# The second value tile of a pair: projected in the step of the causal attention product instead of the step of the first two mixes

## What is computed

```python
def _L0_attn_ref(x, WQ, WK, WV, WO):          # 16 heads of width 16, causal
    Q, K, V = (heads(WQ), heads(WK), heads(WV))
    score = jnp.einsum('bhqd,bhkd->bhqk', Q, K) / jnp.sqrt(jnp.asarray(D_K, x.dtype))
    score = score + mask
    ...
    out = jnp.einsum('bhqk,bhkd->bhqd', score, V)
    ...
    return out @ WO

def _moe_attn(x, Wq, Wk, Wv, Wo, Wsel_v, Wsel_o):   # 16 heads of width 64, 8 experts, top 2
    q = _rope(jnp.einsum('bsd,hdp->bhsp', x, Wq))
    k = _rope(jnp.einsum('bsd,hdp->bhsp', x, Wk))
    gv = _gate(x, Wsel_v)
    v = jnp.einsum('bsd,bhse,hedp->bhsp', x, gv, Wv)
    att = jax.nn.softmax(jnp.einsum('bhsp,bhtp->bhst', q, k) / np.sqrt(P), axis=-1)
    o = jnp.einsum('bhst,bhtp->bhsp', att, v)
    go = _gate(x, Wsel_o)
    return jnp.einsum('bhsp,bhse,hepd->bsd', o, go, Wo)
```

## Time and profile before

| | |
|---|---|
| time, median of 3 runs | 3404.29 us (3403.39 to 3406.31) |
| span of the profiled execution | 3401.4 us |
| TensorE matmul busy | 3233.1 us, 95% |
| VectorE, ScalarE, GpSimd busy | 72%, 58%, 42% |
| mean granted TensorE clock | 0.995 of full speed |
| DMA | 295.18 MB, mean 87 GB/s |

### The profile page before, as it was taken

How to read it: one execution, slowest core, us unless ns; L and a number is a source line. 1 busy time by engine, 2 the same in 40 slices (tenths; PEclk the granted TensorE clock), 3 DMA queues, 4 the chain that set the end, 5 groups by cost and what they waited for, 6 DMA issues and landing times.

```text
span 3401.4 us, 64468 instructions
## 1 busy us (share of the span) xinstructions
PE 3233.1 (95%) x18240; PEld 2378.9 (70%) x18240; DVE 2439.7 (72%) x4708; ACT 1961.5 (58%) x4509; POOL 1441.9 (42%) x1215
## 2 busy tenths in 40 slices
PE   1699999999999999999999999999999999997998
PEld 1577777777777777777777777777777777775765
DVE  6577777777777777777777777777777777775554
ACT  2466666656666666666666666666666666664121
POOL 4144355445443454345543554434534543442212
PEclk9999999999999999999999999999999999999999
DMA  5223333334233333233233332333332433333221
GB/s 165 76 71 87 95 90 85 77 76 109 76 84 87 84 98 81 75 100 96 69 87 76 96 98 77 76 104 81 84 87 68 114 81 75 84 75 110 72 83 62
DMA packets 115937, 295.18 MB, mean 87 GB/s; under 512 B 33856, under 2 KB 54592, under 8 KB 99264
## 3 DMA queue, kind: packets, MB, share of 16 engines
q1 hardware_dynamic: 115904, 294.78, 32.9%
HBM read 262.74 MB, written 31.98 MB: 87 GB/s over the span
## 4 chain that ended last, share of the span: by engine, by line
PE 85%; issue 6%; DVE 5%; ACT 3%; DMA 1%; POOL 0%; ACTq 0%; SPq 0%; DVEq 0%; POOLq 0%
PE bank L673 27%; PE bank L799 22%; PE bank L718 9%; PE bank L773 7%; PE bank L688 5%; PE bank L905 4%; PE bank L897 3%; PE bank L693 3%; PE bank L745 2%; PE bank L754 2%; ACT probs L957 2%; DVE uf L1239 1%; DVE oo L1232 1%; PE bank L694 1%; ACT pt_e L977 1%
## 5 line engine op out<-in xcount | busy, mean ns | idle before, releaser
L573 POOL TENSOR_TENSOR u_l<-uf,u_h 128x512 fp32r<-128x512 f32 x512 | 716.1, 1409 | 722.6 <-ACT u_h L1041 722.4
L1136 DVE TENSOR_REDUCE nmax<-bank 128x1 f32<-128x512 f32 (+3 forms) x1024 | 551.8, 579 | 305.0 <-PE bank L688 297.8
L673 PE MATMUL bank<-wv_h,xx 128*128 128x512 f32 x2048 | 755.0, 410 | 7.1 <-DVE vm L1157 7.1
L957 ACT ACTIVATE probs<-bank,nmax 128x512 f32<-128x512 f32 (+3 forms) x1024 | 590.7, 610 | 253.2 <-DVE nmax L1136 253.1
L1041 ACT ACTIVATE u_h<-uf 128x512 fp32r<-128x512 f32 x512 | 321.7, 632 | 696.9 <-DVE uf L1239 683.6
L673 PEld LDWEIGHTS bank<-wv_h,xx 128*128 128x128 f32 x2048 | 386.0, 188 | 155.8 <-issue 59.6
L718 PEld LDWEIGHTS bank<-ident_sb,probs 128*128 128x128 f32 x3328 | 388.3, 141 | 106.4 <-issue 51.3
L718 PE MATMUL bank<-ident_sb,probs 128*128 128x128 f32 x3328 | 451.3, 274 | 1.6 <-ACT stackT L1032 0.9
L569 POOL TENSOR_TENSOR v_sb<-v_next,zero_hb 128x512 f32<-128x512 f32 x64 | 74.2, 1160 | 891.9 <-PE bank L773 877.4
L799 PE MATMUL bank<-u_h,wo_h 128*128 128x512 f32 x1024 | 427.1, 417 | 5.0 <-ACT u_h L1041 3.2
L1239 DVE TENSOR_TENSOR uf<-oo,go 128x512 f32<-128x512 f32 x512 | 416.2, 823 | 8.8 <-POOL u_l L573 6.6
(11 more groups left out here) (141 smaller groups left out, 5164.2 us busy)
## 6 DMA issues: line engine op xcount, KB each, us to landing
go<-go_d SPq DMA_DIRECT2D x256, 512.0 KB, 6.5
xx<-xs_d SPq DMA_DIRECT2D x128, 512.0 KB, 3.5
oo<-scale_d SPq DMA_DIRECT2D x128, 128.0 KB, 2.9
a_d<-a_out SPq DMA_DIRECT2D x128, 128.0 KB, 2.3
pt_c<-in_x SPq DMA_DIRECT2D x16, 512.0 KB, 4.7
st<-in_wv SPq DMA_DIRECT2D x16, 512.0 KB, 5.8
st<-in_wo SPq DMA_DIRECT2D x16, 512.0 KB, 7.2
go_d<-go_turned SPq DMA_DIRECT2D x256, 8.0 KB
```

What stands on the lines that cost most here:

```text
L573: nc.gpsimd.tensor_tensor(u_l[:, e % 2], uf[:, e % 2], u_h.bitcast(f32)[:, e % 2], ALU.subtract).then_inc(ul_done, 1)
L673: last = nc.tensor.matmul(out, lhs, rhs, start=n == 1, stop=n == 3 * len(chunks))
L957: nc.scalar.activation(probs[:, s % 2, j, 0:w], sbank[j][:, 0:w], ACT.Exp, bias=nmax[:, 2 * s + j:2 * s + j + 1], **kw).then_inc(exp_done, 1)
L1136: nc.vector.tensor_reduce(nmax[:, 2 * s + j:2 * s + j + 1], sbank[j][:, 0:w], AX.X, ALU.max, negate=True).then_inc(nmax_ready, 1)
```

## The change

One entry moves in the table of TensorE's jobs: V1 is issued in step 1, behind V0 and ahead of `turn(1)` and of the scores of step 3, and no longer in step 2 between J0 and J1. The tables of the other engines stay as they are, and so does the order of the jobs that share the two banks.

```diff
 PE_FILL = [[("P", 0), ("P", 1), ("P", 2), ("P", 3), ("AT", 0)],
-           [("AC", 0), ("V", 0)],
-           [("J", 0), ("V", 1), ("J", 1)],
+           [("AC", 0), ("V", 0), ("V", 1)],
+           [("J", 0), ("J", 1)],
            [("V", 2), ("J", 2), ("J", 3)],
            [("V", 3), ("J", 4), ("V", 4)],
            [("QK", 0), ("J", 5), ("QK", 1)],
```

## The result

The changed kernel takes 3443.43 us, median of 4 runs (3441.99 to 3445.84), against 3404.09 us for the kernel before (4 runs): ratio 1.0113, 95% interval 1.0099 to 1.0127. Predicted were 3445.8 us. The profiled execution's span is 3444.0 us, 42.6 us over that of before.

A forecast was written before the change was run, and what follows sets the result against it. TensorE was taken to bound the kernel, with one hole per pass. 0.81 us longer less 0.14 given back, 62 times, adds 41.5 us to span 3401.4; plus 2.9 gives 3445.8 us, range 3430 to 3461.

The forecast's parts named there:

- The bound and the place: TensorE bounds the loop, one 0.59 us wait per pass before L693; moved V1 waits for the a_out copy's bank release.
- The six pieces: TensorE from V0's end to turn(2): V1's wait, V1, turn(1), scores(3), J0, J1; 5.62 us before, 6.43 us after.
- The weight load: At V1: its first load stays uncovered behind the unmet wait, so V1 takes 1.48 us, not 1.39.
- What was given back: At J2 and J3: 0.14 us per pass of waiting for u_l and an uncovered load goes away.
- The tie at u_h: At the u_h copy of mix 2: J0 ends about when its data is ready, at worst 0.1 us late, off the path.
- The sum: Whole loop: 0.81 - 0.14 = 0.67 us per pass, 62 passes, 41.5 us added to the span.
- The 2.9 us: Whole run: the median of the runs taken to lie 2.9 us over the profiled span.
- The first pass: Loop's first pass: V1's bank is free and V1 fills part of a 3.25 us hole; taken as 0, at best 1.4 us gained.
- V1 fills the hole: Rival, before L693: V1 covers the 0.74 us hole if its bank is free; about 46 us gained, 3358 us; 4%.
- The clock: Rival, at V1's wait: the longer pauses lower the granted clock, 1.16 us per pass, 72 us in all, 3518 us; 3%.
- the new pause is shorter than one that had left the clock alone: Argument against a clock drop at V1: its 1.46 us pause is shorter than a late 2.36 us one with clock 1.00.

The follow-up runs named there:

- The run with the copy first: Changed kernel, with ScalarE's copy of the causal product to a_out (L1037) moved ahead of the exponentials of step 2: 3404.65 us.
- The runs with the hole filled: Changed kernel with the a_out copy ahead of step 2's exponentials, 3404.65 us; kernel before with J0 instead of V1 moved to step 1, 3402.36 us.

## Why the prediction was right, and where it was not

- **The bound and the place.** TensorE with one hole per pass, and V1 on the bank of the causal product: shown, by the waits of the changed kernel and by the pair of runs with the copy made twice (36 us on one kernel, some 30 of them the copy's own, and nothing on the other).
- **The six pieces.** Predicted 6.43 us; measured 1650.23 - 1648.77 = 1.46 (wait, predicted 1.46), 1.52 (V1, 1.48), 0.21 (turn(1), 0.24), 0.31 (scores, 0.33), 1.49 (J0, 1.50), 1.40 (J1, 1.42), together 6.39. V1 is the only piece longer than predicted.
- **The weight load.** V1's load was not pulled ahead while the wait stood: it starts at 1650.23, after 1.73 us of idle time, and V1 takes 1.52 us, not 1.39. The early load that the Trainium skill describes ("TensorE: Matmul & The Clock Gate", what happens when a matmul is issued) does not reach past a wait that is not met: V1's load has 106.5 us of idle time before it in 62 passes. An unmet wait is not the only thing that keeps a load late. J0 waits for nothing either, but its first load starts only 0.02 us ahead of its first matmul (1652.25), and J0 takes 1.49 us; J2's starts 0.22 us ahead (1658.29), and J2 takes 1.41.
- **What was given back.** J2 to turn(3) took 2.95 us and takes 2.81: the 0.14 us. The tie at u_h came out as forecast, 4.46 us behind the copy's start against 4.41.
- **The sum.** 0.67 us per pass was predicted. The one pass shown gives 6.39 - 5.62 - 0.14 = 0.63, the mean over all is 0.61. That is 38 us instead of 41.5. Nearly all of the rest of the 42.6 us between the spans lies ahead of the loop, where I had put 0: the first copy to a_out starts at 186.2 instead of 181.0. So it is luck that the spans, 42.6 us apart, come so near to 41.5; the medians are 3443.43 - 3404.09 = 39.3 us apart. The 2.9 us that I added for the median over the span were those of one execution: the profiled execution of the changed kernel took 3445.84 us with a span of 3444.0, 1.8 us less, and it was the slowest of the four.
- **The first pass.** I took 0, at best a gain. TensorE had already come 1.2 us later to this pass, before any moved instruction. V1 then filled part of the first hole, a new hole of 2.08 us stood before the scores of step 4, as they could not pass the exponentials, and the clock stayed low for longer: at the level of 1.2 GHz from about 142.7 to 149.5 us, before from 140.9 to 144.3. Windows 140 to 150 and 170 to 180 us of the changed kernel and then of before (length; PE, PEld, DVE, ACT, POOL busy; granted clock; DMA share, GB/s):

```profile
140.00:150.00 10.00, 6.17 (x25) 4.26 (x26) 8.66 (x20) 5.75 (x17) 0.68 (x1) 0.66 0.00 0
...
170.00:180.00 10.00, 7.75 (x33) 5.50 (x33) 1.86 (x7) 2.28 (x5) 0.00 (x0) 0.83 0.43 87
```
```profile
140.00:150.00 10.00, 9.41 (x45) 7.18 (x46) 9.38 (x19) 5.13 (x17) 0.68 (x1) 0.83 0.00 0
...
170.00:180.00 10.00, 10.00 (x64) 5.82 (x63) 6.31 (x15) 3.71 (x8) 2.87 (x3) 1.00 0.21 44
```

  The longer stretch at the lower level cost about 1.2 us (from the scores of step 4 to those of step 5 4.40 us instead of 3.24), a longer wait for a DMA (2.25 instead of 0.95 us) another 1.3, and the lower clock behind that wait some 1.5. The run with the copy first has V1 in the same place and nearly the same holes in this pass (1.92 and 2.01 us) with a clock of 0.66 over 140 to 150 us, but neither the long DMA wait nor the low clock behind it. So the 1.2 us go with V1's place, and the last 2.8 us do not follow from it alone. These are single executions, and the first copy starts anywhere from 179.5 to 186.9 us in the other profiles.
- **The rival that was mispriced.** I gave "V1 fills the hole" 46 us of gain. The runs with the hole filled show 0 to 3 us. The step that fails is the point where I let the whole 0.74 us through and only said that J3's 0.14 might not be given back. The row that I had used for J3 says that its u_l is done at 1636.13, and nothing that TensorE does between AC and J2 makes it earlier; TensorE arriving 0.74 us earlier can only wait there. I read that slack in one direction, for a delay, and not in the other, for a gain.
- **The clock.** The 62 pauses of 1.3 us did not lower the level: from 180 to 3100 us the granted clock is 1.00, over the whole and in each window of 10 us. The one drop near the loop's start (0.83 over 170 to 180 us) follows the wait for the DMA. The window 180 to 3100 us of the changed kernel:

```profile
180.00:3100.00 2920.00, 2836.92 (x16576) 2106.50 (x16572) 2244.74 (x4021) 1817.34 (x4208) 1279.10 (x1124) 1.00 0.32 84
```

  The reason that I gave, that the new pause is shorter than one that had left the clock alone, does not hold. With the copy twice the pause is 1.78 us, still shorter than 2.36, and the clock fell in five passes. So what the rival describes begins to show with 0.48 us more of waiting, at 1.6 us for each pass in which it happened.

## What to carry to other kernels

Before a job is moved into a hole of the bounding engine, write down what it waits for at the new time, its PSUM bank above all, and compare the end of that release with the start of the hole: here the release came 0.48 us after the end of the hole that it was to fill. A hole is worth only the way to the next wait behind it, so the gain of filling it needs the slack of the next inputs, and two limits that hide each other look worthless when tried one at a time (3 us, not clear of nothing, and 6 us apart, 55 us together).

## What the runs showed of the hardware

A pause of 2.36 us late in the span had left the granted clock at 1.00, and I argued from its length. The changed kernel has a shorter one, 2.25 us, in its first pass, and the clock fell. TensorE behind this pause:

```profile
173.43 0.66 PE L673 MATMUL bank<-wq_h,xx 128*128 128x384 f32 x1 [2.25 <-DMA xx<-xs_d]
173.89 0.52 PE L673 MATMUL bank<-wq_l,xx 128*128 128x384 f32 x1
...
176.96 0.34 PE L673 MATMUL bank<-wq_h,xx 128*128 128x384 f32 x1
```

Matmuls of this shape take 0.52 us at first and 0.34 us some 3 us later, at the two levels of 1.2 and 2.4 GHz; the granted clock over 170 to 180 us is 0.83 (the window above). So the length of a pause alone does not tell whether the level drops. Of the pauses at V1, one per pass in an engine that is else busy, those of 1.3 us (changed kernel, every 47.2 us) lowered it in none of 62 passes, and those of 1.78 us (copy twice, every 47.7 us) in five of 62; each time this cost about 1.6 us. What sets these five apart from the other 57 is open.
